# Three key chunks split by GpSimd's transfers instead of by ScalarE and VectorE, in a cross-attention block on one core

## The reference

```python
Sim = (encoder_hc @ w1)[:, :, None] + (decoder_hq @ w2)[:, None, :] + jnp.einsum('bid,bjd->bij', encoder_hc * w3, decoder_hq) + b_sim[0]
A = jax.nn.softmax(Sim, axis=2)
hq_hat = jnp.einsum('bij,bjd->bid', A, decoder_hq)
Batt = jax.nn.softmax(jnp.max(Sim, axis=2), axis=1)
hc_bar = jnp.einsum('bi,bid->bd', Batt, encoder_hc)[:, None, :]
feats = jnp.concatenate([encoder_hc, hq_hat, encoder_hc * hq_hat, encoder_hc * hc_hat], axis=-1)
hcq = feats @ W_qv + b_qv
```

## Time and profile before

| | us |
|---|---|
| runs, median (lowest to highest) | 120.96 (118.67 to 121.33) |
| the profiled execution, its own time | 120.4 |
| its span in the trace | 118.1 |
| key phase, until the last maximum | about 45.3 |
| row phase | 45.3 to about 92.6 |
| tail | 92.6 to 118.1 |

### The profile page before, as it was taken

One profiled execution on the slowest core, in us unless ns is written; L12 is line 12 of the kernel. 1 busy time (PEld: TensorE's weight loads), 2 busy tenths in 40 slices (PEclk: granted clock), 3 DMA queues, 4 the chain that ended last, 5 costly groups with the idle time before them and its releaser, 6 DMA issues.

```text
span 118.1 us, 1714 instructions
## 1 busy us (share of the span) xinstructions
PE 111.0 (94%) x561; PEld 85.1 (72%) x563; DVE 92.5 (78%) x142; ACT 69.6 (59%) x125; POOL 25.8 (22%) x34
## 2 busy tenths in 40 slices
PE   5799999999999999999999999999999999999780
PEld 2257676767676777698999898998989675865370
DVE  1667999999999999999989899999997321542541
ACT  5075748475464626999997979888877102021220
POOL 2100000000000745057643643525310010000100
PEclk9999999999999999999999999999999998599999
DMA  3999999999999999999999999100000000000001
GB/s 108 347 373 416 413 412 409 409 411 411 409 395 412 433 391 412 409 409 442 405 392 418 404 416 363 40 0 0 0 0 6 0 0 0 0 0 0 0 0 47
DMA packets 8073, 29.27 MB, mean 248 GB/s; under 512 B 1025, under 2 KB 1281, under 8 KB 7810
## 3 DMA queue, kind: packets, MB, share of 16 engines
q1 hardware_dynamic: 7920, 29.17, 62.4%
q10 hardware_dynamic: 146, 0.01, 0.1%
HBM read 29.04 MB, written 0.13 MB: 247 GB/s over the span
## 4 chain that ended last, share of the span: by engine, by line
PE 43%; DVE 21%; issue 20%; DMA 7%; ACT 3%; SPq 2%; POOLq 1%; POOL 0%; DVEq 0%; ACTq 0%
PE mixed_ps L760 18%; DVE neg_scores L538 12%; PE mixed_ps L762 9%; PE scores_ps L731 9%; DMA raw<-keys_dram 7%; DVE pair L516 6%; PE side_ps L775 2%; SPq L332 2%; ACT neg_scores L403 1%; PE scores_ps L881 1%; ACT pair L384 1%; PE scores_ps L674 1%; PE scores_ps L887 1%; PE scores_ps L768 1%; PE scores_ps L767 1%
## 5 line engine op out<-in xcount | busy, mean ns | idle before, releaser
L516 DVE TENSOR_TENSOR pair<-raw,pair 128x1024 fp32r<-128x1024 f32 (+1 forms) x42 | 51.0, 1227 | 2.4 <-ACT pair L384 2.3
L384 ACT ACTIVATE pair<-raw 128x512 fp32r<-128x512 f32 (+1 forms) x42 | 34.1, 813 | 18.5 <-DMA raw<-keys_dram 15.0
L368 POOL CAST pair<-raw 128x512 fp32r<-128x512 f32 x23 | 23.4, 1020 | 58.3 <-DMA raw<-rows_dram 37.5
L760 PE MATMUL mixed_ps<-pair,turned_high 128*128 128x512 f32 x88 | 33.8, 417 | 0.1
L762 PE MATMUL mixed_ps<-pair,turned_low 128*128 128x256 f32 x88 | 24.7, 281 | 0.0
L760 PEld LDWEIGHTS mixed_ps<-pair,turned_high 128*128 128x128 f32 x88 | 16.5, 188 | 3.3 <-issue 0.3
L545 DVE TENSOR_TENSOR turned_low<-scores_ps,turned_high 128x512 fp32r<-128x512 f32 (+1 forms) x24 | 16.2, 674 | 1.0 <-ACT turned_high L416 0.5
L762 PEld LDWEIGHTS mixed_ps<-pair,turned_low 128*128 128x128 f32 x88 | 16.7, 190 | 0.0
L538 DVE TENSOR_SCALAR_CACHE_REDUCE neg_scores<-scores_ps,neg_max 128x1024 f32<-128x1024 f32 (+2 forms) x14 | 16.1, 1147 | 0.4
L731 PE MATMUL scores_ps<-ident,neg_scores 128*128 128x128 f32 x98 | 14.8, 273 | 0.3 <-ACT neg_scores L403 0.2
L403 ACT ACTIVATE neg_scores<-neg_scores,neg_max 128x1024 f32<-128x1024 f32 (+2 forms) x15 | 14.3, 954 | 1.4 <-DVE neg_scores L538 1.4
(11 more groups left out here) (141 smaller groups left out, 91.0 us busy)
## 6 DMA issues: line engine op xcount, KB each, us to landing
raw<-keys_dram SPq DMA_DIRECT2D x24, 512.0 KB, 8.7
raw<-rows_dram SPq DMA_DIRECT2D x24, 512.0 KB, 8.1
w<-weights_dram SPq DMA_DIRECT2D x1, 1792.0 KB, 11.3
w<-weights_dram SPq DMA_DIRECT2D x1, 1024.0 KB, 9.5
const<-const_dram SPq DMA_DIRECT2D x1, 320.0 KB, 11.7
raw<-keys_last_dram SPq DMA_DIRECT2D x1, 256.0 KB, 8.1
raw<-rows_last_dram SPq DMA_DIRECT2D x1, 256.0 KB, 4.6
x_sb<-x_dram SPq DMA_DIRECT2D x1, 128.0 KB, 2.1
```

Source lines behind the costliest of these rows:

```text
L368: nc.gpsimd.tensor_copy(out=pair[:, use % PAIR_BUFS, 0, 2 * D:4 * D], in_=raw[:, slot(item), 2 * D:4 * D])\
L384: nc.scalar.activation(pair[:, use % PAIR_BUFS, 0, 0:columns], raw[:, slot(item), 0:columns], ACT.Copy)\
L516: nc.vector.tensor_tensor(out=pair[:, use % PAIR_BUFS, 1, 0:columns], in0=raw[:, slot(item), 0:columns], in1=pair[:, use % PAIR_BUFS, 0, 0 ...
L760: nc.tensor.matmul(mixed_ps[:, :].rearrange("p (h d) -> p h d", h=2), probs_high, both[:, :, t * D:(t + 1) * D], start=(k == EARLY and t = ...
```

## The change

Five chunks are native now, 0, 4, 8, 11 and 24. Three chunks, 13, 17 and 21, are *fetched*: SP does not load them, and neither ScalarE nor VectorE splits them. GpSimd issues a transfer from HBM that rounds the chunk to float32r on its way (the high half), ScalarE writes the negated high half into the place of the low half, and GpSimd issues a second transfer of the same chunk that adds to it, so that the low half stands there. The other seventeen are split as before. The fetched halves stand in the space of `turned_high` and `turned_low`. A fetch starts when `pair_used` shows that scores(k-7) are done, and the third also waits until the first buffer has been used. The negation stands in ScalarE's order ahead of the high half of chunk k-3. TensorE multiplies a fetched chunk like a split one.

```diff
+NATIVE = (0, 4, 8, 11, 24)
+FETCHED = (13, 17, 21)
+FETCH_LEAD = 7
...
     def is_native(k):
 
-        return k % 4 == 0
+        return k in NATIVE
...
+        fetched = [buf[:, :, :].rearrange("p (h b) n -> p h (b n)", h=2) for buf in (turned_high, turned_low)]
...
-            for k in range(CHUNKS):
-                wait_for_slot(k)
+            for k in ring_chunks:
+                item = key_item[k]
+                wait_for_slot(item)
...
+            def fetch_high(fetch):
+
+                k = FETCHED[fetch]
+                pool.wait_ge(pair_used, split_before[k - FETCH_LEAD + 1])
+                if fetch >= 2:
+                    pool.wait_ge(fetched_used, fetch - 1)
+                nc.gpsimd.dma_start(out=fetched[fetch % 2][:, 0, :], in_=keys_full[k]).then_inc(fetched_high, 16)
+
+            def fetch_low(fetch):
+
+                pool.wait_ge(fetched_negated, fetch + 1)
+                nc.gpsimd.dma_start(out=fetched[fetch % 2][:, 1, :], in_=keys_full[FETCHED[fetch]], accum_op=ALU.add)\
+                    .then_inc(fetched_low, 16)
+
+            for fetch in range(len(FETCHED)):
+                fetch_high(fetch)
+                fetch_low(fetch)
             for k in range(EARLY, FULL):
...
+            def negate_fetched(fetch):
+                act.wait_ge(fetched_high, 16 * (fetch + 1))
+                both = fetched[fetch % 2]
+                nc.scalar.activation(both[:, 1, :], both[:, 0, :].bitcast(F32), ACT.Copy, scale=-1.0)\
+                    .then_inc(fetched_negated, 1)
...
             for k in range(2, CHUNKS):
-                if not is_native(k):
+                if k + 3 in FETCHED:
+                    negate_fetched(FETCHED.index(k + 3))
+                if is_split(k):
                     keys_high(k)
...
+                elif is_fetched(last):
+                    dve.wait_ge(fetched_used, FETCHED.index(last) + 1)
...
+                if is_fetched(k):
+                    fetch = FETCHED.index(k)
+                    high, low = fetched[fetch % 2][:, 0, :], fetched[fetch % 2][:, 1, :]
+                    pe.wait_ge(fetched_high, 16 * (fetch + 1))
+                    for a in range(DH):
+                        nc.tensor.matmul(out_ps, q_high[:, a, :], keys_part(high, k, a), start=(a == 0), stop=False)
+                    for a in range(DH):
+                        nc.tensor.matmul(out_ps, q_low[:, a, :], keys_part(high, k, a), start=False, stop=False)
+                    pe.wait_ge(fetched_low, 16 * (fetch + 1))
+                    for a in range(DH):
+                        last = nc.tensor.matmul(out_ps, q_high[:, a, :], keys_part(low, k, a), start=False,
+                                                stop=(a == DH - 1))
+                    last.then_inc(fetched_used, 1)
+                    return
```

More of the change, by code:

```diff
@@ L71, in is_native, with is_fetched, is_split, row_item @@
     def is_native(k):
-        return k % 4 == 0
+        return k in NATIVE
+    def is_fetched(k):
+        return k in FETCHED
+    def is_split(k):
+        return not is_native(k) and not is_fetched(k)
     native_before = [sum(is_native(j) for j in range(k)) for k in range(CHUNKS + 1)]
-    split_before = [k - native_before[k] for k in range(CHUNKS + 1)]
+    split_before = [sum(is_split(j) for j in range(k)) for k in range(CHUNKS + 1)]
     KEY_SPLITS = split_before[CHUNKS]
+    ring_chunks = [k for k in range(CHUNKS) if not is_fetched(k)]
+    KEY_ITEMS = len(ring_chunks)
+    key_item = {k: item for item, k in enumerate(ring_chunks)}
+    def row_item(k):
+        return KEY_ITEMS + k
     def row_use(k):
@@ L236, in build @@
         native_done = sem("native_done")
+        fetched_high = sem("fetched_high")
+        fetched_negated = sem("fetched_negated")
+        fetched_low = sem("fetched_low")
+        fetched_used = sem("fetched_used")
         max_done = sem("max_done")
@@ L565, in _ @@
                 for k in chunks:
-                    if k + 2 < CHUNKS and not is_native(k + 2):
+                    if k + 2 < CHUNKS and is_split(k + 2):
                         keys_low(k + 2)
@@ L687, in scores @@
                 if is_native(k):
-                    pe.wait_ge(loaded[slot(k)], loads(k))
+                    pe.wait_ge(loaded[slot(key_item[k])], loads(key_item[k]))
                     for a in range(DH):
@@ L738, in mix_early @@
                     pe.wait_ge(max_done, eviction_of[22] + 2)
-                pe.wait_ge(loaded[slot(CHUNKS + k)], loads(CHUNKS + k))
+                pe.wait_ge(loaded[slot(row_item(k))], loads(row_item(k)))
                 pe.wait_ge(early_turned, k + 1)
@@ L742, in mix_early @@
                     last = nc.tensor.matmul(early_ps, turned_early[:, k, t * P:(t + 1) * P],
-                                            rows_tile(raw[:, slot(CHUNKS + k), :], t), start=(k == 0 and t == 0),
+                                            rows_tile(raw[:, slot(row_item(k)), :], t), start=(k == 0 and t == 0),
                                             stop=(k == EARLY - 1 and t == TILES - 1))
```

30 lines of the change are left out of this document (15 added, 15 removed).

## The result

136.41 us, median of 4 runs (135.93 to 137.41), against 120.61 us for the kernel before (4 runs, 118.67 to 121.33): ratio 1.143, 95% interval 1.126 to 1.160. By the medians the change makes the kernel 15.8 us slower. The ratio is taken over the quicker runs of each kernel only (of the kernel before 118.67 and 120.26 us), and by these the change costs 17.1 us, while the profile of the kernel before, 120.4 us, is one of its slower runs. I had forecast 8.1 us more, and a range up to 136.0.

The account below looks back on a forecast made before the run. VectorE and TensorE in balance bound the key phase, TensorE the row phase. Three loops of 8.46 us put the last maximum at 53.3 instead of 45.25 us: 120.4 + 8.1 = 128.5 us, range 120.0 to 136.0.

Parts of the forecast that it names:

- three loops end to end: Key phase: scores(10) and (14) ending start the fetches of chunks 17 and 21; three loops of 8.46 us in sequence.
- H: Time from the end of scores(k-7) until the fetched high half is in SBUF: 4.5 us, ends 2.1 to 8.4.
- the rest of the loop: After the high half lands: negation 1.06, high half of k-3 1.06, subtraction 1.22, TensorE's last pair 0.62; 3.96 us.
- rival four: GpSimd's high transfer queues behind SP's backlog, so its time to landing nears 8.4 us: 140 us, chance 5%.
- Only its last pair is on the loop: Within the loops a slow TensorE clock is hidden; after the last loop up to 0.9 us, not added.
- The traffic at nothing: Net 1.5 MB more DMA, 3.8 us at 410 GB/s, costed at nothing since row chunks come 6 us early.
- The prize: One VectorE subtraction fewer in the key phase: 1.1 us saved if everything new stayed hidden.
- Rival two: The adding transfer takes 7.0 us and delays the next high half in two loops: 132.5 us, chance 20%.
- Rival three: VectorE keeps GpSimd from issuing its transfers, up to 2.4 us more, three times: 135.7 us, chance 8%.
- Rival one: High transfer within 1.8 us never holds ScalarE's queue: 119.3 us; chance 10% with run spread, 15% more within 2%.
- Nothing for row phase and tail: After the key phase, the row phase and tail follow unchanged in length: 0 us.

Follow-up runs that it names:

- experiment 11: Changed kernel without its transfers and negations, buffers zeroed by GpSimd: 123.64 us; last run, buffers filled by ScalarE from x: 118.88 us, ratio 1.001.
- experiment 1: Kernel before plus six 512 KB GpSimd transfers after its end, on an idle chip: plain 3.9 and 3.5 us, rounding 3.6 and 3.4, adding 5.3 and 5.4.
- experiment 2: Changed kernel with SP's eleventh load held back until the first high half has landed: 139.51 us, first transfer 3.8 us.
- experiment 4: Changed kernel with dummy matmuls ahead of scores 10, 14 and 18: 136.51 us, with more of them 136.46 us; an unchanged repeat 135.78 us.
- experiment 10: Kernel before plus unused GpSimd transfers: six, three of them adding, 146.12 us, clean version 129.13; six without adding 124.94; last run, three rounding, 119.82.
- experiment 9: Changed kernel with two fetched chunks, 14 and 20, six native, high transfers issued early after scores(1) and (3): 122.9 us, ratio 1.037.
- experiment 5: Changed kernel with the second transfer of each fetch rounding instead of adding: 135.47 us, ratio 1.142.

## Why the prediction was wrong

The direction, the mechanism and the place were right: ScalarE waits ahead of each negation, TensorE at the first matmul of scores 10, 14 and 18, three loops end to end, low halves in time. The size was off by 7.4 us against the profiled execution, and by 9.0 us as a difference (17.1 against 8.1), in part since the 120.4 us that I started from had a tail 1.9 us longer than the 28.3 of experiment 11:

| term | forecast | measured |
|---|---|---|
| start, end of scores(6) | 18.16 | 18.70 |
| H (end of scores(k-7) to the negation), three loops | 4.5 each, 13.5 | 7.47, 5.83, 6.75, sum 20.05 |
| the rest of the loop, three | 3.96 each, 11.9 | 5.05, 4.53, 5.04, sum 14.62 |
| from scores(18) to the last maximum | 9.8 | 9.15 |
| last maximum ends | 53.3 | 62.52 |
| row phase, tail and what lies around the span | 0 | -1.7 together |

- **H, the failed step** (+6.6 us of the 9.2 in the key phase). I took 1.9 us fixed and 2.56 of data at half share. The half share is nearly right (56 to 49%, 3.1 us), the fixed part was not: behind SP's loads the first data come after 4.0 us, on idle engines after 1.2 to 1.6 (experiment 1), and with the loads held back the whole transfer takes 3.8 (experiment 2). This was my rival four, a transfer that queues behind the backlog, at a little over half the way (mean 6.7 us, between my 4.5 and its 8.4), and I gave it 5%. I had 8.4 us in the rows as the upper end and set it aside "since the queues are different ones". It did not queue behind the whole backlog either: it started late and then had half. The second and third transfers, 5.5 and 6.4 us, share the engines with the low transfer ahead of them on their own queue (27.55 + 6.1 and 38.41 + 5.3 us run past 31.52 and 41.89); that this is why they took longer than the 3.6 is argued, not shown.
- **"Only its last pair is on the loop"** (+2.7 us). True at 2.4 GHz, where the rest of a loop was 4.04 us (experiment 4). But the first matmul of chunk k-3 waits for its high half too, so all three pairs stand behind the wait, and at 1.2 GHz they take 2.9 us (28.32 to 31.22), where I had 1.22 for the subtraction and 0.62 for the last pair. In the third loop this hardly lengthens the key phase, since VectorE ends it: hence 9.15 instead of 9.8 in the table. Keeping the clock up gave 1.5 us back in the first two loops, and the transfers took 1.8 us longer (experiment 4).
- **The traffic at nothing.** Nearly right for this kernel, for the wrong reason. Net bytes cost 1.3 us by themselves (the last run of experiment 10), but in the changed kernel the stalls seem to let the ring fill again: from 14 to 62 us ScalarE waits for ordinary keys for 1.9 us in all. I looked at the slack of the row chunks and should have looked at that of the keys: the bus runs at 410 GB/s through the whole key phase, so each extra transfer eats the keys' cushion. In a version without stalls it decides (experiment 9).
- **The prize, 1.1 us.** It is 0 (experiment 11). A subtraction saved where TensorE has no lead is a wait of VectorE.
- **Rival two, the adding transfer binds.** That adding is dearer was right, though by less than its 7.0 us (5.3 to 6.1 us in place, 5.3 to 5.4 against 3.6 alone); that it binds was not: TensorE's need comes later, and without the adding the time is nearly the same (experiment 5). The Trainium skill (Collectives: The Full Stack, The bandwidth ceiling, on why ReduceScatter is half of AllGather) says that an addition needs two source reads; the traces agree, with 292 to 346 GB/s instead of 410 where adding transfers run (experiments 9 and 10).
- **Rival three** is refuted by experiment 2 for the first transfer, the one that it tests. **Rival one** would have needed H under 2 us; the quickest of these transfers on an idle chip took 3.4.
- **Nothing for row phase and tail**: right, +0.5 us in the row phase; the tail's -1.8 us come of a fall of the clock in the profile before, and the run without fetches has a tail of 28.3 us as well.

## What to carry to other kernels

Before a transfer goes onto a second queue, look at how many loads stand in the first: with full engines the time from issue to landing is set by the backlog as well as by the bytes (7.1 us here against 3.6), and every step that waits for it in an engine's order must have that much lead. Where an engine waits in its own order and a later event of the same loop triggers the next wait, multiply the miss by the number of loops. And measure the prize with the new cost taken away before building the rest: here a saved subtraction was worth nothing, since two engines were in balance.

## What the runs showed of the hardware

- A transfer by GpSimd that rounds float32 to float32r on its way takes no longer than a plain one (3.4 and 3.6 against 3.5 and 3.9 us for 512 KB); one that adds to SBUF takes 5.3 to 5.4 us, and while such transfers run the full engines move 292 to 346 GB/s instead of 410.
- Behind full hardware queues the first data of such a transfer come 4.0 us after its issue; on idle engines after 1.2 to 1.6 us.
- GpSimd's clearing of two buffers stretched VectorE's two layer norm instructions from 0.60 to 3.60 us.
- One 16 KB code packet (queue "q8 instruction", 1.1 us on one DMA engine) fell into the first transfer in two runs, both with more matmuls in the code: the last four or so of its 144 packets came 1.5 us late, and it landed after 8.6 and 8.7 us instead of 7.1. In the ten comparable runs that have none there it landed after 7.1 or 7.2 us; the packet was not varied by itself.
